# A first stage in another order, and 16-bit fill products on TensorE where other stages begin and in the router

## The reference

```python
...
x = x + tanh(g_xattn[0]) * xattn0(layernorm(x), ctx)      # q, k, v with biases, 16 heads of 16, then relu(out @ W1 + b1) @ W2 + b2
x = x + tanh(g_ffn[0]) * ffn0(layernorm(x))               # fp4(silu(fp4(x) @ fp4(w_gate)) * (fp4(x) @ fp4(w_up))) @ fp4(w_down)
x = x + tanh(g_xattn[1]) * xattn1(layernorm(x), ctx, mask) # no biases, then out @ Wo
x = x + tanh(g_ffn[1]) * moe1(layernorm(x))               # softmax gate, top 2 of 8, sum of gate * (relu(x @ W1 + b1) @ W2 + b2)
...
```

## Time and profile before

| what | us |
|---|---|
| median of 3 runs (lowest, highest) | 739.69 (739.12, 741.12) |
| profiled execution | 739.43 |
| its span in the profile | 737.70 |
| PE busy, DVE busy | 590.7, 542.5 |
| ACT busy, POOL busy | 348.6, 250.2 |

### The profile page before, as it was taken

The page is one execution under the profiler, slowest core; times in us unless marked ns, Lnnn a source line. Parts: engine busy times, 40 slices in busy tenths (PEclk is TensorE's granted clock), DMA queues, the critical chain, the costliest instruction groups (busy, mean ns, idle before and its releaser), DMA issues. The chain is left out here.

```text
span 737.7 us, 15590 instructions
## 1 busy us (share of the span) xinstructions
PE 590.7 (80%) x5555; PEld 527.1 (71%) x5555; DVE 542.5 (74%) x1117; ACT 348.6 (47%) x865; POOL 250.2 (34%) x253
## 2 busy tenths in 40 slices
PE   4559999899624799999966999998662999999950
PEld 3238999799513688888865899987661889989940
DVE  5958898668995699999882778886568764555537
ACT  2256776523135545554432656555154555555520
POOL 2536767800200000000010556665202475555420
PEclk9999999999955799999996899999655899999985
DMA  8020000030000000000000000000394122222229
GB/s 233 4 65 1 4 2 3 2 118 0 1 0 0 1 1 1 0 1 1 1 1 0 2 2 2 2 4 2 119 381 149 46 80 79 79 74 80 70 73 308
DMA packets 27637, 36.75 MB, mean 50 GB/s; under 512 B 4024, under 2 KB 22265, under 8 KB 27438
## 3 DMA queue, kind: packets, MB, share of 16 engines
q1 hardware_dynamic: 23822, 25.56, 10.7%
q0 software_dynamic: 3744, 10.23, 4.5%
HBM read 26.47 MB, written 9.31 MB: 49 GB/s over the span
## 5 line engine op out<-in xcount | busy, mean ns | idle before, releaser
L940 POOL TENSOR_TENSOR rstd<-mv,eps_col 128x16 f32<-128x16 f32 (+2 forms) x6 | 1.3, 209 | 263.1 <-DVE mv L472 263.1
L970 POOL TENSOR_TENSOR p_lo<-prob,p_hi 128x616 f16<-128x616 f32 x64 | 87.1, 1362 | 5.1
L964 POOL CAST p_hi<-prob 128x616 f16<-128x616 f32 x64 | 44.6, 696 | 68.3 <-ACT prob L1093 68.3
L1021 POOL DMA_INDIRECT y_rows<-rn,dst_row x39 | 43.1, 1106 | 54.8 <-DVE rn L889 53.6
L1093 ACT ACTIVATE prob<-prob 128x616 f32<-128x616 f32 x64 | 45.9, 718 | 32.9 <-DVE prob L575 32.9
L1101 ACT ACTIVATE pT<-ps 128x512 f32<-128x512 f32 (+1 forms) x96 | 46.8, 522 | 25.8 <-PE ps L1426 25.4
L575 DVE TENSOR_TENSOR prob<-ps,smax 128x308 f32<-128x308 f32 x128 | 55.3, 474 | 2.2
L1017 POOL DMA_INDIRECT xin<-x_rows,src_row x39 | 38.2, 979 | 52.6 <-DVE dst_row L856 41.0
L461 DVE CAST ehT_hi<-ehid 128x512 fp32r<-128x512 f32 x39 | 16.6, 427 | 53.0 <-ACT ehid L1317 52.7
L570 DVE TENSOR_REDUCE smax<-ps 128x8 f32<-128x616 f32 x64 | 50.5, 790 | 0.8 <-PE ps L1410 0.8
L1303 ACT ACTIVATE eh<-ps 128x512 f32<-128x512 f32 x39 | 23.3, 597 | 57.6 <-PE ps L1342 57.5
(11 more groups left out here) (282 smaller groups left out, 2013.9 us busy)
## 6 DMA issues: line engine op xcount, KB each, us to landing
el_w<-in_L_ffn_W_dram SPq DMA_DIRECT2D x16, 512.0 KB, 9.8
eh_w<-y_rows SPq DMA_DIRECT2D x16, 256.0 KB, 5.9
x_sb<-in_x_dram SPq DMA_DIRECT2D x4, 512.0 KB, 8.1
x_rows<-rn SPq DMA_DIRECT2D x4, 512.0 KB, 10.1
out_dram<-x_sb SPq DMA_DIRECT2D x16, 128.0 KB, 3.6
stage<-in_L_xattn_W_dram SPq DMA_DIRECT2D x2, 512.0 KB, 3.9
...
```

The costliest lines, as they stand in the source:

```text
L964: pool.tensor_copy(p_hi[:, t % 2, c], prob[:, t % 2, c]).then_inc(s["hi"], 1)
L970: pool.tensor_tensor(p_lo[:, t % 2, c], prob[:, t % 2, c], p_hi[:, t % 2, c], ALU.subtract).then_inc(s["lo"], 1)
L1021: pool.indirect_dma_start(y_rows, bass.IndirectOffsetOnAxis(ap=dst_row[:, j:j + 1], axis=0), ey[:, j % YRING], None) .then_inc(y_out[j % Y ...
```

## The change

**Loads**: the context and Wk come first, then the small constants; a table that nothing uses is no longer loaded; `c_spread` and the first chunk of x have semaphores of their own. **Values**: ScalarE casts a value block out of PSUM to the first bf16 part, TensorE subtracts that part in PSUM with a negated fp16 identity (`value_less`); what is left is cast and subtracted again, and cast a third time; the five VectorE calls per block are gone. **Keys** of layer 1 have other PSUM banks. **Tables**: ScalarE does layer 1's first 14, VectorE the other 6. **Moments**: only tiles 0 to 3 are in the first stage; those of 4 to 15 and their rows on GpSimd (`early_rows`) stand inside the first attention, those of tiles 4 to 7 ahead of `mlp_weights`. Two weight splits move from VectorE to GpSimd. **Fills**: `keep_warm(bank, count)` issues bf16 products of ones, 128x512, into an unused bank: 6 at barrier 2, 12 and 1 ahead of the first two transposes of the FFN, 10 at barrier 6, one per tile in the router, 10 and 1 around the first transpose of the experts.

```diff
@@ -375,24 +376,23 @@
...
     xt = I["x"].rearrange("b (t p) d -> p (b t) d", p=P)
-    sp.dma_start(ident[:, :], I["c_ident"]).then_inc(ld["const"], 16)
-    sp.dma_start(head_mask[:, :, :], I["c_head"].rearrange("p (j s) -> p j s", s=NH_MAX)).then_inc(ld["const"], 16)
-    sp.dma_start(k_mask[:, :], I["c_kmask"]).then_inc(ld["const"], 16)
-    sp.dma_start(stage_sel[:, :], I["c_sel"]).then_inc(ld["const"], 16)
     sp.dma_start(ctxT[:, :, :], I["ctxT"].rearrange("(k p) m -> p k m", p=CP)).then_inc(ld["ctx"], 16)
...
     sp.dma_start(bk_col[:, :], I["L0_xattn_bk_cols"]).then_inc(ld["k"], 16)
+    sp.dma_start(k_mask[:, :], I["c_kmask"]).then_inc(ld["const"], 16)
+    sp.dma_start(ident[:, :], I["c_ident"]).then_inc(ld["const"], 16)
+    sp.dma_start(head_mask[:, :, :], I["c_head"].rearrange("p (j s) -> p j s", s=NH_MAX)).then_inc(ld["const"], 16)
     for n in range(2):
...
     sp.dma_start(bv_row[:, :], I["L0_xattn_bv"].rearrange("(a n) -> a n", a=1)).then_inc(ld["v"], 16)
-    sp.dma_start(stage[0:M, 2:5, :].rearrange("p a n -> p (a n)")[:, 0:HM], I["c_spread"]).then_inc(ld["v"], 16)
+    sp.dma_start(stage[0:M, 2:5, :].rearrange("p a n -> p (a n)")[:, 0:HM], I["c_spread"]).then_inc(kp["table"], 16)
     for n in range(2):
...
     for c in range(4):
-        sp.dma_start(x_sb[:, 4 * c:4 * c + 4], xt[:, 4 * c:4 * c + 4]).then_inc(ld[f"x{c}"], 16)
+        sp.dma_start(x_sb[:, 4 * c:4 * c + 4], xt[:, 4 * c:4 * c + 4]).then_inc(ld["x1" if c else "x0"], 16)
     sp.dma_start(gates[:, 0:2], I["g_xattn"].rearrange("(a n) -> a n", a=1).broadcast_to([P, 2])).then_inc(ld["bias"], 16)
...
@@ -480,11 +480,16 @@
...
     assert ch.n == 6
-    dve.wait_ge(ld["const"], 64)
+    dve.wait_ge(ld["const"], 48)
+    dve.wait_ge(kp["zero"], 1)
+    for j in range(PT):
+        dst = vbd[:, :, :, j, 0, :].rearrange("p a b (s c) -> p (a b) s c", c=SLOT)[:, :, :, HD]
+        ch.done(dve.tensor_copy(dst, bcast(head_mask[:, j, :], 1, 2 * B)))
     for n in range(2):
...
             dve.wait_ge(kp["k_ready"], 2 * n + hf + 1)
-            src = ps[:, hf, 0:B * M]
+            src = ps[:, 4 * n + hf, 0:B * M]
...
-            dve.tensor_copy(v3[:, g, 2], v_rest[:, 1]).then_inc(kp["v3_ready"], 1)
-    dve.wait_ge(kp["zero"], 1)
-    for j in range(PT):
-        dst = vbd[:, :, :, j, 0, :].rearrange("p a b (s c) -> p (a b) s c", c=SLOT)[:, :, :, HD]
-        ch.done(dve.tensor_copy(dst, bcast(head_mask[:, j, :], 1, 2 * B)))
+    dve.wait_ge(ld["x0"], 16)
+    for t in range(SOON):
+        moments(t)
+    aggregate(0, last=SOON)
+    hi, lo, at = splits[0]
+    dve.wait_ge(act_done, 1)
+    ch.done(dve.tensor_tensor(lo, stage[:, at], two_parts(hi), ALU.subtract))
     for g in range(B):
...
             at = g * PT + j
-            if at < TILES:
-                if at % 4 == 0:
-                    dve.wait_ge(ld[f"x{at // 4}"], 16)
-                moments(at)
-            elif at == TILES:
-                aggregate(0)
             dve.wait_ge(kp["b_ready"], at + 1)
...
             dst = vbd[0:ROWS[j], 0, g, j, :, 0:nh * SLOT].rearrange("p c (s d) -> p c s d", s=nh)[:, :, :, 0:HD]
-            dve.tensor_tensor(dst, src, hm, ALU.mult).then_inc(kp["b_used"], 1)
-    for n, (hi, lo, at) in enumerate(splits):
-        dve.wait_ge(act_done, n + 1)
-        ch.done(dve.tensor_tensor(lo, stage[:, at], two_parts(hi), ALU.subtract))
+            ins = dve.tensor_tensor(dst, src, hm, ALU.mult)
+            if at >= ACT_BLOCKS:
+                dve.wait_ge(kp["c_ready"], at + 1)
+                src = ps[0:ROWS[j], 6 + at % 2, 0:3 * nh * HD].rearrange("p (c s d) -> p c s d", c=3, s=nh)
+                dst = vbd[0:ROWS[j], 1, g, j, :, 0:nh * SLOT].rearrange("p c (s d) -> p c s d", s=nh)[:, :, :, 0:HD]
+                ins = dve.tensor_tensor(dst, src, hm, ALU.mult)
+            ins.then_inc(kp["b_used"], 1)
     dve.wait_ge(ld["bias"], 48)
...
@@ -625,6 +619,17 @@
...
                 aggregate(3, last=EARLY)
+            if n == 0 and k == -2:
+                dve.wait_ge(ld["x1"], 48)
+                for t in range(SOON, 2 * SOON):
+                    moments(t)
+                aggregate(0, first=SOON, last=2 * SOON)
+            if n == 0 and k in (0, 1, 3, 4):
+                for t in range(8 + k // 3 * 4 + k % 3 * 2, 10 + k // 3 * 4 + k % 3 * 2):
+                    moments(t)
+            if n == 0 and k in (1, 4):
+                g = 2 + k // 4
+                aggregate(0, first=SOON * g, last=SOON * (g + 1))
...
@@ -940,19 +945,26 @@
...
-    pool.wait_ge(ld["const"], 64)
+    pool.wait_ge(ld["const"], 48)
+    def shift_rows(k, n, part, first=0, last=TILES):
+        pool.wait_ge(rs[n], part)
+        ch.link(pool.tensor_tensor(shift_a[:, k, first:last], mv[:, n, first:last, 0], rstd[:, n, first:last], ALU.mult))
+        pool.tensor_scalar(shift_a[:, k, first:last], shift_a[:, k, first:last], -1.0, None, ALU.mult).then_inc(rs[n], 1)
+    def early_rows(g):
+        inverse_deviation(0, g + 1, first=SOON * g, last=SOON * (g + 1))
+        shift_rows(0, 0, 2 * g + 1, first=SOON * g, last=SOON * (g + 1))
+    pool.wait_ge(kp["kT_ready"], 2)
     for hf in range(2):
-        pool.wait_ge(kp["kT_ready"], hf + 1)
         for b in range(B):
...
                 spread_keys(pool, 1, hf, b, hi)
-    def shift_rows(k, n, part):
-        pool.wait_ge(rs[n], part)
-        ch.link(pool.tensor_tensor(shift_a[:, k], mv[:, n, :, 0], rstd[:, n], ALU.mult))
-        pool.tensor_scalar(shift_a[:, k], shift_a[:, k], -1.0, None, ALU.mult).then_inc(rs[n], 1)
-    inverse_deviation(0)
-    shift_rows(0, 0, 1)
+    early_rows(0)
+    for n, (hi, lo, at) in enumerate(splits):
+        if n:
+            pool.wait_ge(act_done, n + 1)
+            pool.tensor_tensor(lo, stage[:, at], two_parts(hi), ALU.subtract)
     barrier(pool, 1)
...
@@ -971,6 +983,8 @@
...
         for t in range(TILES):
+            if n == 0 and t in (3, 6):
+                early_rows(2 + t // 6)
             if t:
...
@@ -987,6 +1001,7 @@
...
+    early_rows(1)
     mlp_weights(0, w1_hi, w1_lo)
...
@@ -1034,15 +1049,24 @@
...
     credits(act, [fs_[n] for n in "xnorm xmag hmag xhi xlo silu hthi htlo".split()])
-    act.wait_ge(ld["v"], 64)
+    act.wait_ge(ld["const"], 48)
+    act.activation(ident_h[:, :], ident[:, :], ACT.Copy)
+    act.activation(neg_ident[:, :], ident[:, :], ACT.Copy, scale=-1.0)
+    act.activation(less_h[:, :], ident[:, :], ACT.Copy, scale=-1.0)
+    act.wait_ge(kp["table"], 16)
     act.activation(spread[:, :], stage[0:M, 2:5, :].rearrange("p a n -> p (a n)")[:, 0:HM], ACT.Copy)\
         .then_inc(kp["spread"], 1)
+    for g in range(2 * B):
+        act.wait_ge(kp["v_ready"], g + 1)
+        act.activation(v3[:, g, 0], ps[0:M, V_BANK[g], 0:D], ACT.Copy).then_inc(kp["cast"], 1)
     act.wait_ge(ld["q"], 64)
...
         act.activation(hi, stage[:, at], ACT.Copy).then_inc(act_done, 1)
-    act.wait_ge(ld["const"], 64)
-    act.activation(ident_h[:, :], ident[:, :], ACT.Copy)
-    act.activation(neg_ident[:, :], ident[:, :], ACT.Copy, scale=-1.0)
+    for part in range(1, 3):
+        for g in range(2 * B):
+            act.wait_ge(kp["rest"], 2 * B * (part - 1) + g + 1)
+            act.activation(v3[:, g, part], ps[0:M, V_BANK[g], 0:D], ACT.Copy)\
+                .then_inc(kp["cast"] if part == 1 else kp["v3_ready"], 1)
     act.wait_ge(ld["bias"], 48)
...
@@ -1050,6 +1074,8 @@
...
             at = g * PT + j
+            if at >= ACT_BLOCKS:
+                continue
             act.wait_ge(kp["c_ready"], at + 1)
...
@@ -1064,6 +1090,8 @@
...
             att_wait(act, n, "xt", p)
+            if n == 0:
+                act.wait_ge(rs[0], 2 * (2 * p // SOON + 1))
             for k in range(2):
...
@@ -1346,22 +1375,34 @@
...
         for hf in range(2):
-            if n:
-                pe.wait_ge(kp["k_used"], hf + 1)
             for k in range(KC):
-                ins = pe.matmul(ps[:, hf, 0:B * M], wk[:, n, k, hf * P:(hf + 1) * P], ctxT[:, k], start=(k == 0), stop=(k == KC - 1))
+                ins = pe.matmul(ps[:, 4 * n + hf, 0:B * M], wk[:, n, k, hf * P:(hf + 1) * P], ctxT[:, k], start=(k == 0), stop=(k == KC - 1))
             ins.then_inc(kp["k_ready"], 1)
-    pe.wait_ge(ld["v"], 64)
+    def value_block(g):
+        n, b = g // B, g % B
+        o = ps[0:M, V_BANK[g], 0:D]
+        for k in range(KC):
+            ins = pe.matmul(o, ctxT[:, k, b * M:(b + 1) * M], wv[:, n, k], start=(k == 0), stop=(n == 1 and k == KC - 1))
+        if n == 0:
+            ins = pe.matmul(o, ones_f[:, :], bv_row[:, :], start=False, stop=True)
+        ins.then_inc(kp["v_ready"], 1)
+    def value_less(g, part):
+        pe.wait_ge(kp["cast"], 2 * B * part + g + 1)
+        pe.matmul(ps[0:M, V_BANK[g], 0:D], less_h[0:M, 0:M], v3[:, g, part], start=False, stop=True, skip_group_check=True)\
+            .then_inc(kp["rest"], 1)
+    pe.wait_ge(ld["v"], 48)
     pe.wait_ge(dve_done, 6)
-    for n in range(2):
-        for b in range(B):
-            g = 2 * n + b
```

(30 more changed lines are left out.)

25 lines of the change are left out of this document (9 added, 16 removed).

## The result

The changed kernel takes 729.63 us (median of 4 runs, 728.74 to 731.36), the kernel before 739.45 in the same session: ratio 0.9854, 95% interval 0.9827 to 0.9880 (the two medians alone give 0.9867). The profiled execution is the slowest of the four, 731.36 us, so the trace explains 8.1 us.

What follows compares the result with a forecast made beforehand. TensorE was taken to set the first attention's pace, with 8.6 us of slack on VectorE and 18.6 on GpSimd. The terms summed to -7.4 us from the profiled 739.43: 732.0 us, range 726.5 to 738.5.

Steps and rivals of the forecast that it cites:

- First stage: Start to first normalise: value split off VectorE, earlier products and shared tables open the barrier at 37.5, not 46.1: -8.6 us.
- GpSimd's order: Start of first attention: rows of tiles 4 to 7 ahead of the MLP weight split delay the first high half: +3.2 us.
- Inserted work: First attention: added VectorE moments and GpSimd rows mostly fit in slack, part surfaces: +0.9 us, ends 0 and 8.2.
- The clock fall there: First attention: TensorE's longer pause may bring the half clock once more: +1.2 us, ends 0 and 2.9.
- MLP: Six fills at the barrier to the MLP keep the clock up, at 0.35 us delay: -1.1 us in all.
- FFN: Twelve fills hidden in TensorE's wait; half the possible clock gain counted, as sparse work follows them: -0.6 us.
- Router: Ten fills raise the clock, tiles come 0.85 us apart, ScalarE's expert conversions limit the gain: -2.1 us.
- the rival given 0.14: Router: clock rises, then falls at the first expert conversion while TensorE waits for ScalarE's copies: +1.5 us, 735.6; chance 0.14.
- the slower rival: Router: fills don't raise the clock, tiles 1.60 us apart, +8.2 us instead of -2.1, 743.2 in all; chance 0.10.
- The cap: Router: ScalarE's conversions limit the gain; the third moves from 541.85 to between 539.0 and 540.3, bounded by its load.
- Experts: Eleven fills around the experts' first transpose, ten hidden; a long pause before the gather limits the gain: -0.3 us.
- the rule's own sum: Fills stopping before dense work need not keep the clock: FFN and experts give 0, whole change -6.5 us, 732.9.

Runs made afterwards that it cites:

- the swap: The changed kernel with GpSimd's split of the MLP weight put ahead of the rows of tiles 4 to 7 again: 728.59 us, ratio 0.9826.
- the moments' move: The changed kernel with the moments of tiles 4 to 11 moved into VectorE's table loop of the first stage: 728.15 us, ratio 0.9842.
- the warm start: 18 more TensorE fills at the first attention's start, on the changed kernel with all tiles' rows done ahead of that attention: 721.55 us, ratio 0.9729.

## Why the prediction was right, and where its steps were not

**First stage: the mechanism right, the size wrong.** Forecast -8.6 with ends of -5 and -10; measured -15.1 with the clock up and -11.6 without (46.14 to 34.52), both outside these ends. Two terms were mis-sized. The value blocks were put at 20.5 for their end, from the load order before; they ended at 14.6 (at half clock near 19). And "the weight splits 1.9, eight casts 3.2" stood behind one another; eight casts took 2.26. So v was ready at 18.7, not 25.8. Of the 5.9 us by which the values ended early 4.6 are the clock's (19.17 against 14.59). From v to the first normalise the sum was near: 11.7 forecast, 12.3 measured. The clock at 9.4 was in no step. The profile of before shows 0.29 us between key products and a pause at their fourth group, and nines in the first slices though these products ran at half; I did not ask what the removed wait would do to the clock. The parts measured singly: the value route 10.7 us, the loads 2.6, the wait for the banks 2.7, the clock 3.5. They overlap and don't add.

**GpSimd's order: right.** +3.2 forecast, +2.7 measured; the swap gave 1.7 of it back, the moments' move 1.9. The other 0.8 are not GpSimd's: they are what the high half is late (13.91 against 13.14) in the kernel before with fills alone, where the order is the old one and the clock came up later than in the trace before.

**Inserted work: the step that named the wrong engine.** I weighed VectorE's 0.6 us a tile and took GpSimd's 18.6 us of slack in the 76 us as cover. It is an average: at the start GpSimd is behind, and its two groups of rows stand in that part. +0.9 forecast, 88.66 - 86.45 = +2.2 measured from the first probability transposes to the end of the attention, in the traces in which the clock did not fall. Moving VectorE's calls for tiles 4 to 11 left it (88.61); moving GpSimd's rows and VectorE's last four moments took it away (86.67). The upper end of 8.2 should have been 8.5 (4.5 + 4), which changes nothing.

**The clock fall there: right where it happens.** +1.2 forecast; 1.5 to 1.8 us between the traces with it (108.8 to 109.1) and without (107.32).

**MLP: the price right, in half of the executions.** -1.1 forecast. From GpSimd's first MLP work to VectorE's first call of the weight preparation it takes 50.17 and 49.94 us in the two traces without these fills. In six of the twelve with them the clock stays up and it takes 48.9, 1.1 less on average; in the other six, the trace after among them, the half stretch is there all the same and it takes 50.1 to 50.5. So the mean is -0.4. The step had the clock's price and missed that in some executions the clock falls just as the fills begin (in the trace after at 139.11, with the first fill at 138.92). (The whole piece up to the FFN is 0.9 shorter on average, 85.6 us against 86.60 and 86.38; the other half of that lies in the weight preparation, where no fill stands.)

**FFN: wrong.** -0.6 forecast, +0.7 in the trace after; over all traces no gain is to be seen. In the trace after the clock came up on the fills and was down again when the dense products came, the case that the step left open.

**Router: forecast and rival both.** -2.1 forecast; -2.6 in the trace after. Over the ten traces with one fill per tile it took 17.07 to 20.92 us, mean 18.8: -1.8. In six of them the clock held to the last tile (17.07 to 18.63 us); in four it fell back while TensorE waited for ScalarE (19.58 to 20.92), the rival given 0.14. It is not another outcome of the change but one of its executions. (Against the slower rival I had counted fewer busy microseconds than half in the router's stretch; 29.41 of 54.38 us are more than half.) The cap was foreseen at ScalarE's conversions; their start is set by the load (0.73 us of waiting), which I had as a bound.

**Experts: right on average.** -0.3 forecast. From the first gather to the first hidden tile the twelve traces with these fills take 9.92 to 11.32 us, mean 10.4, the two without 10.69 and 10.64: -0.25. The -0.77 of the trace after is the best of them.

The rule of the Trainium skill quoted ahead ("TensorE: Matmul & The Clock Gate", Part 1: the monitor runs free of the kernel, the point of change differs from run to run) had no row then. Now it has: with the same first-stage code the clock first changes at 9.40 us in one trace and at 49.21 in another, four value products take 1.12 or 1.91 us, and the stage ends at 31.0 or 34.52. The same part of the Trainium skill gives half a microsecond either way for sustained matmuls; in this kernel, whose first stage is not sustained work, it is 40 us. The measured sum of the fills is 1.9 to 2.4 us; the rule's own sum had given them 3.2, the forecast 4.1.

**Not foreseen at all:** the FFN's body took 151.46 instead of 148.84. TensorE was at half clock for 27.31 us on end from 378.04; in the trace before, two stretches of 6.8 and 13.6 us stood there with full clock between. Five of the eleven traces with FFN fills have it (151.4 to 151.5), and the three without (148.84, 148.73, 149.27) don't; three cases are too few to blame the fills. This is open. In three of the five the next piece is 0.8 us shorter, which is the -0.79 of the table.

A version that beats both came of it: rows ahead of the attention (ratio 0.9775), and with the warm start 0.9729, 19 to 20 us less than the kernel before.
